# Local attention on one Trainium2 core: the band copied by VectorE, shifted rows fetched by SyncE transfers

## The reference

```python
def _layer(x, ...):                      # DIM 128, HEADS 8, DIM_HEAD 64, WINDOW 64
    h = shift_token(x)                   # channels 64.. come from the token before
    q, k, v = split(h @ wqkv)            # 8 heads of 64
    q, k = l2norm(q) * qs, l2norm(k) * ksc
    q, k = rotary_xpos(q, k)
    # each window of 64 queries sees its own 64 keys and the 64 before
    sim = einsum('bhwid,bhwjd->bhwij', q * 8, k)
    sim = where((i < j) | (i > j + WINDOW), -max, sim)   # the band
    o = softmax(sim) @ v
    x = x + o @ wo
    ...                                  # layer norm of shift_token(x), gated feed-forward, residual
```

## Time and profile before

| | |
|---|---|
| median of three runs (lowest, highest) | 2616.02 us (2614.52, 2618.11) |
| the profiled execution, its own time | 2621.16 us |
| its span, from the first to the last instruction | 2619.4 us |
| mean granted TensorE clock | 0.954 of full speed |
| PE, DVE, ACT, POOL busy, share of the span | 91%, 68%, 70%, 61% |
| local-attention steps | 4 stages of 64, of which 4 times 56 in the hardware loops |

### The profile page before, as it was taken

How to read it: one execution, slowest core, us unless ns; L and a number is a source line. 1 busy time by engine, 2 the same in 40 slices (tenths; PEclk the granted TensorE clock), 3 DMA queues, 4 the chain that set the end, 5 groups by cost and what they waited for, 6 DMA issues and landing times. The chain is left out here.

```text
span 2619.4 us, 65393 instructions
## 1 busy us (share of the span) xinstructions
PE 2371.7 (91%) x21430; PEld 1658.1 (63%) x21430; DVE 1789.9 (68%) x3820; ACT 1828.4 (70%) x6004; POOL 1605.5 (61%) x1532
## 2 busy tenths in 40 slices
PE   5496999997297899999999999897999999999998
PEld 3494666664295677764677764573677764677753
DVE  2394788884295788864788864684788864888864
ACT  3253788883153899983899983435899983999982
POOL 2672677770673788870888860330888860888860
PEclk7797899998698999999999999999999999999999
DMA  6111000000112000000000000000000000000000
GB/s 270 45 49 43 1 1 0 0 1 0 46 49 100 2 0 0 0 0 1 2 0 0 0 0 1 1 0 1 2 0 0 0 1 0 2 0 0 0 1 33
DMA packets 20372, 42.70 MB, mean 16 GB/s; under 512 B 4016, under 2 KB 14256, under 8 KB 19472
## 3 DMA queue, kind: packets, MB, share of 16 engines
q1 hardware_dynamic: 15696, 31.71, 3.4%
q0 software_dynamic: 4544, 9.35, 1.1%
HBM read 24.45 MB, written 16.59 MB: 16 GB/s over the span
## 5 line engine op out<-in xcount | busy, mean ns | idle before, releaser
L272 POOL TENSOR_TENSOR l_tS<-l_t,tabs 128x512 f32<-128x512 f32 x256 | 326.5, 1275 | 225.1 <-DVE l_t L361 216.2
L276 POOL TENSOR_TENSOR l_t<-l_t,l_tS 128x512 f32<-128x512 f32 x256 | 401.6, 1569 | 23.9 <-POOL l_tS L272 7.6
L299 ACT ACTIVATE l_pr<-psum,l_nm 128x128 f32<-128x128 f32 x1024 | 361.2, 364 | 47.2 <-DVE l_nm L365 38.4
L360 DVE TENSOR_TENSOR l_t<-psum,tabs 128x512 f32<-128x512 f32 x256 | 176.9, 691 | 205.5 <-POOL l_t L276 187.9
L267 POOL TENSOR_TENSOR l_pr<-l_pr,l_rl 128x512 f32<-128x512 f32 x256 | 266.6, 1042 | 54.7 <-DVE l_rl L355 23.8
L343 DVE SCALAR_TENSOR_TENSOR l_qk<-l_rn,l_t 128x512 f32<-128x512 f32 x256 | 277.7, 1085 | 8.9 <-ACT l_rn L331 5.1
L168 PE MATMUL psum<-l_hT,big 128*128 128x256 f32 x1024 | 266.9, 383 | 18.6 <-DVE l_t L361 18.4
L876 POOL TENSOR_TENSOR ss_pr<-ss_pr,ss_rl 128x256 f32<-128x256 f32 (+1 forms) x256 | 221.4, 886 | 91.1 <-DVE ss_rl L979 89.0
L191 PE MATMUL psum<-l_sq,cf 128*128 128x512 f32 x512 | 263.9, 597 | 0.0
L922 ACT ACTIVATE ss_pr<-psum,ss_nm 128x128 f32<-128x128 f32 (+1 forms) x512 | 210.5, 444 | 9.1 <-DVE ss_nm L972 9.1
L299 ACT ACTIVATION_READ_ACCUMULATOR l_pr<-psum,l_nm 128x1 f32 x1024 | 207.0, 202 | 0.0
(11 more groups left out here) (180 smaller groups left out, 5498.0 us busy)
## 6 DMA issues: line engine op xcount, KB each, us to landing
big<-early SPq DMA_DIRECT2D x1, 6688.0 KB, 37.2
ex_xb<-sorted SPq DMA_DIRECT2D x78, 64.5 KB
z<-token_y SPq DMA_DIRECT2D x16, 256.0 KB, 6.7
sorted<-z SPq DMA_DIRECT2D x2, 1999.5 KB, 18.4
big<-late SPq DMA_DIRECT2D x1, 3114.0 KB, 10.3
cf<-const SPq DMA_DIRECT2D x1, 2089.5 KB, 12.4
x<-x_t SPq DMA_DIRECT2D x4, 512.0 KB, 7.1
x_final<-x SPq DMA_DIRECT2D x1, 2048.0 KB, 7.0
```

The lines of the kernel that those rows point to most:

```text
L272: pool.tensor_tensor(tS[:, :], t2[:, :], tab[:, 1, :], ALU.mult).then_inc(ts_ready, 1)
L276: pool.tensor_tensor(t3[:, j % 2, :], t1[:, :], tS[:, :], ALU.add).then_inc(summed, 1)
L299: ins = act.activation(pr[:, (j - 3) % 2, h, t * P:(t + 1) * P], s_ps[h][:, t * P:(t + 1) * P], ACT.Exp, bias=nm[:, (j - 3) % 2, h, t:t + ...
```

## The change

Four things are altered, all for `local_attention`.

- The band is written into the two score banks by one VectorE copy (source `band_q`, bf16 in SBUF, read twice; 128 partitions by 512 elements into PSUM) in place of the two identity products. It stands between the probability copy and the reciprocal, after the wait for `p_ready`.
- The sums-of-squares product is split in 384 and 128 columns, and TensorE waits for the normalised q and k and for the band (`qk_ready`, `masked`) ahead of the second piece.
- The rows of a batch come into `hT` by two SyncE transfers (64 partitions each, 64 KB) in place of the two GpSimd copies; a transfer waits until the v projection no longer needs the buffer. TensorE waits for them with `h_there`.
- `t1` has two buffers. L360 now waits for the sum of two steps before and for `ts_ready`, the end of L272 of the step before, since `t2` is still single.

```diff
@@ -138,11 +138,13 @@
     s_ps, pt_ps = (g.bank[3], g.bank[4]), (g.bank[5], g.bank[6])
     sq, t1, t2, tS, t3, lnn, rn, qk, v, hT = (room[x] for x in ("sq", "t1", "t2", "tS", "t3", "lnn", "rn", "qk", "v", "hT"))
     nm, ls, rl, pr, pt, oT = (room[x] for x in ("nm", "ls", "rl", "pr", "pt", "oT"))
-    h_zero, h_low, h_ready, proj_ready, sq_ready = sem("h_zero"), sem("h_low"), sem("h_ready"), sem("proj_ready"), sem("sq_ready")
+    h_zero, proj_ready, sq_ready = sem("h_zero"), sem("proj_ready"), sem("sq_ready")
+    h_there = [sem(f"h_there{k}") for k in range(2)]
     shuffled, ts_ready, summed, ss_ready, ln_ready = sem("shuffled"), sem("ts_ready"), sem("summed"), sem("ss_ready"), sem("ln_ready")
     rn_ready, qk_ready, s_ready, nm_ready, p_ready = sem("rn_ready"), sem("qk_ready"), sem("s_ready"), sem("nm_ready"), sem("p_ready")
     rl_ready, normed, pt_ready, pt_low, pt_high = sem("rl_ready"), sem("normed"), sem("pt_ready"), sem("pt_low"), sem("pt_high")
     vp_ready, v_ready, ol_ready, o_ready, wo_ready, z_ready = sem("vp_ready"), sem("v_ready"), sem("ol_ready"), sem("o_ready"), sem("wo_ready"), sem("z_ready")
+    masked = sem("masked")
     mm = nc.tensor.matmul
 
     def tokens(x, b):
@@ -153,13 +155,25 @@
         for k in range(2):
             for j in range(CH):
                 yield CH * (2 * i + k) + j, 2 * i + k, k, j
+
+    def sync(sp):
+        for b in range(B):
+            z, h = tokens(g.z, b), hT[:, b % 2, :]
+            if b % 2 == 0:
+                prev.there(sp, b // 2)
+            if b >= 2:
+                sp.wait_ge(vp_ready, CH * (b - 1))
+            sp.dma_start(h[0:64, :], z[0:64, :]).then_inc(h_there[b % 2], 16)
+            sp.dma_start(h[64:P, 1:T], z[64:P, 0:T - 1]).then_inc(h_there[b % 2], 16)
 
     def tensor(pe):
         def body(i):
             for s, b, k, j in steps(i):
                 if runs(s, U):
-                    pe.wait_ge(h_ready, b + 1)
+                    pe.wait_ge(h_there[k], 32 * (i + 1))
                     if is_first(s):
+                        if layer == 0:
+                            pe.wait_ge(h_zero, 1)
                         prev.free(pe, 0)
                         pe.wait_ge(g.late_loaded, 16)
                     if at_least(s, 1):
@@ -188,18 +202,17 @@
                         prev.free(pe, 1)
                     if at_least(u, 1):
                         pe.wait_ge(ln_ready, u)
-                    mm(ss_ps[:, :], g.head64[:, :], sq[:, (j - 1) % 2, :], start=True, stop=True).then_inc(ss_ready, 1)
+                    mm(ss_ps[:, 0:3 * P], g.head64[:, :], sq[:, (j - 1) % 2, 0:3 * P], start=True, stop=True, skip_group_check=True)
+                    if runs(s - 2, U):
+                        pe.wait_ge(qk_ready, s - 1)
+                        pe.wait_ge(masked, s - 1)
+                    mm(ss_ps[:, 3 * P:], g.head64[:, :], sq[:, (j - 1) % 2, 3 * P:], start=True, stop=True, skip_group_check=True).then_inc(ss_ready, 1)
 
                 u = s - 2
                 if runs(u, U):
-                    pe.wait_ge(qk_ready, u + 1)
-                    if is_first(u):
-                        prev.free(pe, 3)
-                        prev.free(pe, 4)
-                    if at_least(u, 1):
-                        pe.wait_ge(p_ready, u)
-                    for h in range(2):
-                        mm(s_ps[h][:, 0:BAND], g.ident[:, :], g.band_q[:, :], start=True, stop=False, skip_group_check=True)
+                    if not runs(s - 1, U):
+                        pe.wait_ge(qk_ready, u + 1)
+                        pe.wait_ge(masked, u + 1)
                     for w, q0, spans in ((0, 0, ((0, 0, P),)), (1, LD, ((0, 0, P),)), (0, P, ((P, P, WIN), (P + WIN, WIN, WIN))), (1, P + LD, ((P, P, P),))):
                         for col, k0, n in spans:
                             for h in range(2):
@@ -247,17 +260,6 @@
         rounds(pe, 1, B // 2, 1, body)
 
     def gpsimd(pool):
-        def carry(b, k):
-            z = tokens(g.z, b)
-            if isinstance(b, int) and b < 3:
-                prev.there(pool, b // 2)
-            if at_least(b, 2):
-                pool.wait_ge(vp_ready, CH * (b - 1))
-            pool.tensor_copy(hT[0:64, k, :], z[0:64, :]).then_inc(h_low, 1)
-            pool.wait_ge(h_low, b + 1)
-            pool.tensor_copy(hT[64:P, k, 1:T], z[64:P, 0:T - 1]).then_inc(h_ready, 1)
-            pool.wait_ge(h_ready, b + 1)
-
         def body(i):
             for s, b, k, j in steps(i):
                 u = s - 3
@@ -265,22 +267,17 @@
                     pool.wait_ge(rl_ready, u + 1)
                     x = pr[:, (j - 3) % 2, :, :].rearrange("p h (t n) -> p (h t) n", t=2)
                     pool.tensor_tensor(x, x, rl[:, (j - 3) % 2, :, :].rearrange("p h t -> p (h t)").unsqueeze(2).to_broadcast([P, 4, P]), ALU.mult).then_inc(normed, 1)
-                if j == 0 and runs(b + 1, B):
-                    carry(b + 1, 1 - k)
                 if runs(s, U):
                     pool.wait_ge(shuffled, s + 1)
                     pool.tensor_tensor(tS[:, :], t2[:, :], tab[:, 1, :], ALU.mult).then_inc(ts_ready, 1)
                     pool.wait_ge(ts_ready, s + 1)
                     if at_least(s, 2):
                         pool.wait_ge(qk_ready, s - 1)
-                    pool.tensor_tensor(t3[:, j % 2, :], t1[:, :], tS[:, :], ALU.add).then_inc(summed, 1)
+                    pool.tensor_tensor(t3[:, j % 2, :], t1[:, j % 2, :], tS[:, :], ALU.add).then_inc(summed, 1)
                     pool.wait_ge(summed, s + 1)
-                if isinstance(s, int) and s == 2 * CH - 1:
-                    prev.there(pool, N // (2 * T) - 1)
         if layer == 0:
             pool.memset(hT[64:P, :, 0:1], 0.0).then_inc(h_zero, 1)
             pool.wait_ge(h_zero, 1)
-        carry(0, 0)
         rounds(pool, 1, B // 2 - 1, 2, body)
         pool.wait_ge(normed, U)
 
@@ -332,6 +329,8 @@
         rounds(act, 1, B // 2, 1, body)
 
     def vector(dve):
+        band = g.band_q.unsqueeze(1).to_broadcast([P, 2, BAND])
+
         def body(i):
             for s, b, k, j in steps(i):
                 u = s - 2
@@ -350,14 +349,22 @@
                 u = s - 3
                 if runs(u, U):
                     dve.wait_ge(p_ready, u + 1)
+                if runs(s - 2, U):
+                    if is_first(s - 2):
+                        prev.free(dve, 3)
+                        prev.free(dve, 4)
+                    dve.tensor_copy(g.bank_pair3[:, :, 0:BAND], band).then_inc(masked, 1)
+                if runs(u, U):
                     if at_least(u, 2):
                         dve.wait_ge(normed, u - 1)
                     dve.reciprocal(rl[:, (j - 3) % 2, :, :], ls[:, (j - 3) % 2, :, :]).then_inc(rl_ready, 1)
                 if runs(s, U):
+                    if at_least(s, 2):
+                        dve.wait_ge(summed, s - 1)
                     if at_least(s, 1):
-                        dve.wait_ge(summed, s)
+                        dve.wait_ge(ts_ready, s)
                     dve.wait_ge(sq_ready, s + 1)
-                    dve.tensor_tensor(t1[:, :], qk_ps[:, :], tab[:, 0, :], ALU.mult)
+                    dve.tensor_tensor(t1[:, j % 2, :], qk_ps[:, :], tab[:, 0, :], ALU.mult)
                     dve.stream_shuffle(t2[:, :], qk_ps[:, :], [lane ^ 16 for lane in range(32)]).then_inc(shuffled, 1)
                 u = s - 2
                 if runs(u, U):
@@ -382,7 +389,7 @@
         last = ((shuffled, U), (ln_ready, U), (o_ready, U), (p_ready, U), (p_ready, U), (pt_low, U), (pt_high, U), (z_ready, B))
         eng.wait_ge(*last[bank])
 
-    return Stage(sync=nothing, tensor=tensor, scalar=scalar, vector=vector, gpsimd=gpsimd, there=there, free=free)
+    return Stage(sync=sync, tensor=tensor, scalar=scalar, vector=vector, gpsimd=gpsimd, there=there, free=free)
 
 
 def pair_order(pos):
@@ -659,7 +666,7 @@
 
         def sb(name, shape):
             return ctx.enter_context(nc.sbuf_tensor(f"l1{g.n}_{name}", shape, F32))
-        shapes = dict(sq=[P, 2, 2 * T], t1=[P, 2 * T], t2=[P, 2 * T], tS=[P, 2 * T], t3=[P, 2, 2 * T], lnn=[P, 2 * T], rn=[P, 2 * T], qk=[P, 2, 2 * T],
+        shapes = dict(sq=[P, 2, 2 * T], t1=[P, 2, 2 * T], t2=[P, 2 * T], tS=[P, 2 * T], t3=[P, 2, 2 * T], lnn=[P, 2 * T], rn=[P, 2 * T], qk=[P, 2, 2 * T],
                       v=[P, CH, 3, P], hT=[P, 2, T], nm=[P, 2, 2, 2], ls=[P, 2, 2, 2], rl=[P, 2, 2, 2], pr=[P, 2, 2, T], pt=[P, 2, 2, T], oT=[P, 2, T],
                       y=[P, 2, len(HCH), W])
         room = {k: sb(k, v) for k, v in shapes.items()}
```

## The result

The changed kernel takes 2641.62 us, median of 4 runs (2640.75 to 2644.80); the kernel before, in the same measurement, 2616.31. The ratio is 1.0095, interval 1.0082 to 1.0107: slower by 1%. The prediction was 2612 with a range of 2560 to 2633, and 0.28 for slower. The time lies outside the range and moved the other way.

The account below looks back on a forecast made before the run. PE and the DVE-POOL loop through single t1 were taken to bound equally at 37.80 us a turn; 28 turns at 37.56 give -6.7, the fill +2.7, together -4.0: 2612 us. Range 2560 to 2633; the forecast's own 2603 to 2633.

Parts of the forecast that it names:

- Pair that matters: VectorE's qk multiply and POOL's products exclude each other; where DVE adds into z (j = 0), multiply waits for L276, step 5.59.
- rival 1: In j = 0 steps the multiply comes before L276; all steps about 4.46 us, 2563 us in all; chance 0.22.
- rival 2: The multiply comes before L276 in one of a turn's two j = 0 steps: 2588 us; chance 0.14.
- Band copy: VectorE's copy of the band into PSUM: 0.68 us in all steps, bounds 0.41 to 1.10.
- rival 4: The band copy too is shut out by POOL, in three steps of four: 2711 us; chance 0.06.
- Transfers: SyncE's 64 KB row transfers, 0 to 6.7 us each, start 13 us before use and are hidden.
- an ordinary step: Steps without the addition into z: bound by PE at 4.44 us, except the first after a long step, 4.26.
- the loop's branch: PE's idle time at the end of each eight-step turn: 0.10 us added to 37.46, giving 37.56.
- The step after the long one: The step following j = 0: from one band copy's end to the next, 4.26 us.
- PE's own step: TensorE's work per step falls from 4.71 to 4.39 to 4.49 us without the identity products; middle 4.44 taken.
- The fill: Start of each of four stages: first scores come 0.68 us later, +2.7 us in all.
- rival theory C: Explanation tested after the result: the transfers, or the extra waits of the split product, are the loss; no chance given.

Follow-up runs that it names:

- run 1: Changed kernel with VectorE's addition into z moved behind the next step's qk multiply: 2575.34 us, 0.9832 of the kernel before.
- run 4: Changed kernel with the band written by two identity products on PE again and L191 undivided; SyncE rows and two t1 buffers stay: 2610.45 us, 0.9964.
- run 5: Kernel before the change with only the addition into z moved behind the next step's qk multiply: 2622.09 us, 1.0010.
- run 10: Changed kernel with the addition into z moved, the band on PE by identity products again and L191 undivided: 2608.99 us, 0.9955.
- run 3: Changed kernel with the rows fetched by the two GpSimd copies again instead of SyncE transfers: 2610.93 us, 0.9973.
- run 6: Kernel before the change with only the VectorE band copy and split product added; t1 single, rows by GpSimd: 2625.08 us, 1.0026.
- run 7: Changed kernel with the addition into z moved and the rows fetched by GpSimd copies again: 2617.24 us, 0.9995.
- run 8: Changed kernel with the addition into z moved and a single t1 buffer again: 2577.57 us, 0.9844.
- run 9: Changed kernel with the addition into z moved and one 512 column sums-of-squares product, all of it waiting for the band: 2846.26 us, 1.0861.
- run 2: Changed kernel with one added wait: in j = 0 steps GpSimd holds L276 until the qk multiply is over; 2583.73 us, 0.9867.

## Why the prediction was wrong

The collision was the right mechanism and it was read off. What failed is the step time of the ordinary steps around it, and with it the sign; the range failed by the stage ends and the base.

**Right.** *Pair that matters.* The multiply was forecast to meet L276 in the j = 0 steps, to end 0.54 after it and to bring the step to 5.59; it does in both of each turn (1.7 us, end +0.54, issued 0.13 after L276 where 0.08 was forecast), and the step is 5.58. Rivals 1 and 2 are out, rival 1 being what run 1 makes of it: 2563 was worked out for it, 2575 measured. *Band copy*: 0.68 forecast, 0.69 measured, while L276 runs (2436.36, above) or not; rival 4 is out. By the Trainium skill ("VectorE: DVE Perf Modes", section "Why PSUM operands drop a tier") an operand in PSUM rules out the mode that needs both SBUF read ports; the trace agrees for a copy into PSUM, with 0.68 to 0.70 us beside POOL and 0.68 to 0.69 without. *Transfers*: hidden; 1.9 us to land against my bound of 6.7. One sign was off: in the three ordinary steps the multiply takes 0.98, 0.81 and 0.71 us and not near 1.1, since in the later two DVE has waited for ACT and issues it when L272 is almost over.

**The failed step is "an ordinary step".** I gave the three ordinary steps of a batch 4.26 + 2 x 4.44 = 13.14 us; they take 4.48 + 4.49 + 4.57 = 13.54, 0.80 more in a turn. The 0.10 for the loop's branch does not show: the two halves of a turn, one with the branch and one without, are equally long within 0.01 us. A turn was to be 37.56 and is 38.27, so a gain of 0.24 became a loss of 0.51 (before, the mean of 24 turns is 37.76). In the spans the forecast was -4.0 us and +20.2 came; of the 24.2 between them the 24 turns of the table are 12.4 + 24 x 0.24 = 18.2, the stage ends 7.1 (8.8 against +2.7 less 1.0 for their share of the turns), the rest -1.0. Another 5.1 us of the miss is that the profiled execution of before stood that far above its median, while the changed kernel's stood at its own. The failed step has two parts, the larger one first.

- *The step after the long one, 4.26 forecast, 4.48 measured.* The chain of DVE and ACT did 4.26. But I let the chain's time stand as the step's time, where the step is the longer of the chain and PE's own round. PE's round began with the end of its wait, and the 0.9 us for which it had stood were not to be had back. The wait of a long step is paid whole.
- *PE's own step, 4.44 forecast, 4.49 to 4.57 measured* (run 1, where PE is never idle, 4.52 in the mean, from 4.71). So 0.19 came off, a little less than the 0.22 of the identity products: the change of tile shape stays (the quarter product and the scores start 0.39 apart at 2432.93, behind a wait, and 0.32 at 2437.50, where the identity products had L202 and L207 0.32 apart), and the 0.03 left over would be the price of the split, which no run takes alone. I had taken the middle of the bounds where the upper one was right. Why one step in four has 0.08 more stays open.

**Mis-sized: the stage ends.** The fill was put at +2.7 us and the drain at nothing; the first eight steps became 6.0 shorter, the last seven and the drain 14.8 longer. In the last seven the same long steps stand. The drain's +1.05 a stage is the wait for the last band copy, shown above. From the last shuffle of the first stage to the first of the second are 94.3 us in the kernel before and in runs 4, 5 and 10, and 95.0 to 95.3 with the copy, in the changed kernel and in runs 1, 3, 6, 7 and 8 (run 9, whose scores come later still, has 96.8). Some 7 us more is PE at 1.2 GHz in two of the four drains. Within one kernel nothing in the rows decides it: in the first stage PE was likewise busy for 2.30 of 4 us and the clock stayed. Across the twelve traces there is a pattern. The clock fell in 6 of 48 drains, all of them in the four kernels in which the last scores wait 1.70 us for the copy (the changed kernel and runs 2, 3 and 6), and in none of the eight others, where that wait is 1.49 us (addition moved) or 0.8 (band on PE). What decides between the four stages of one kernel is open. The shorter fill needs both the rows by SyncE and the second `t1`: the first eight steps of four stages are 143.7 us before, and 136.1 to 141.0 in the five kernels that have both (137.7 in the changed kernel, 141.0 in run 1), but 142.7 in run 3 and 144.2 in run 8, which lack one each. Which wait of the fill it is stays open.

**And the range.** Its upper end, 2633, already had all ordinary steps at 4.49, and its turn of 38.3 (its own terms give 38.22) is what was measured, 38.27. So the turns did not break the range. The 8.6 us beyond it are 3.8 from the stage ends (8.8 against 3 for the fill and 2 for their share of the turns), 5.4 from the base and rounding (the profiled execution of before, 5.1 above the median that the sum was added to), 0.4 from the turns, and -1.0 from the rest. I had seen the 5 us and left them out of the range. Between the forecast and rival 1, 0.08 us was to decide; 0.13 was measured, on the side that I took, and it could as well have gone the other way: some 50 us of the forecast hung on a tenth of a us.

**Was it a bad change?** No part is bad by itself. In the order of instructions in which it was made, rows by SyncE let the multiply run into L276 at full length (run 4 has it too, hidden), and band on DVE takes the slack that hid it; alone, neither costs more than 0.3% (runs 3, 4 and 6). With the addition moved, the two together give 1.7%. The rival theory C is out as a loss of its own: the transfers and the split are in run 1 as well.

## What to carry to other kernels

Where two engines shut each other out, as VectorE's multiply and GpSimd's products do here, list for each collision which of the two is issued first and by how much; where that margin is a few tenths of a us (0.13 in the changed kernel, 0.24 in run 7), treat it as a thing to be set, by moving an instruction that waits for something else from in front of it or by holding the other engine with a wait, since relieving an engine moves it. When two resources stand at the same height, as PE and the loop over `t1` did here, a part of a change measured alone says little about its worth in the whole (rows by SyncE: +31 or -42 us): try the parts together, and try the order beside them. A step's time is the maximum over the engines' own rounds counted from when each was last released. The engine with the longest round does not catch up after a wait (PE in the changed kernel); one with slack does (DVE in run 4, a step of 4.99 and then one of 4.22).

## What the runs showed of the hardware

- The exclusion has a fixed tail: in the rows shown the multiply ends 0.54 or 0.55 us after POOL's product, whether it was issued 0.06 (run 9), 0.13, 0.24 (run 7) or 0.77 us (run 3) after its start. In the changed kernel's trace 250 multiplies start while a POOL product of the rotation runs; 227 end 0.55 after it; the others were issued in its last 0.11 us, take 0.69 as they do alone, and end 0.58 to 0.63 after it. By the Trainium skill ("SBUF — State Buffer", section "Who interferes with whom") the first issued has the ports for its whole instruction; the traces agree wherever the two starts can be told apart (twice, in runs 2 and 5, they lie 0.005 us apart, and the multiply, recorded second, ran first). The other way round, in the changed kernel, a multiply of 0.98 us from 2435.03 ends at 2436.01 and L276 at 2437.13, 1.12 later.
- A copy of 512 bf16 elements a partition from SBUF into f32 PSUM takes 0.68 to 0.70 us in all 256 instances of the changed kernel, 195 of which overlap a POOL product, and is not held up by POOL.
- The loss can spread to every step: with the wait for the band in front of the whole sums-of-squares product instead of behind three quarters of it, every step collided, and 271 us came (run 9), where I had expected some 80.
- The changed kernel shows the granted clock fall to 1.2 GHz in two of four drains, though the last seven steps before them take 33.53 to 33.55 us in all four; why is open. Each fall lasted some 10 us and cost about 3.5.
